# A one-core cross-attention and expert kernel: norms on ScalarE, first operand pairs on two queues, one gate transpose later, and an end in halves

## What is computed

```python
n = layernorm(x)                      # no weights: (x - mean) / sqrt(var + 1e-5)
q, k, v = n @ Wq.T + bq, ctx @ Wk.T + bk, ctx @ Wv.T + bv       # 16 heads of 8
A = where(causal, q @ k.T / sqrt(8), -inf)                      # per batch and head, 256 x 256
x = x + softmax(A) @ v @ Wo.T + bo
n = layernorm(x)
shared = sum_s gelu(n @ up_s.T) @ down_s.T                      # 2 experts of 64
p = softmax(n @ router.T); gate = p at its top 4 of 16, else 0
routed = sum_r (gate_r * gelu(n @ up_r.T)) @ down_r.T           # 16 experts of 64
x = x + shared + routed
```

## Time and profile before

| what | us |
|---|---|
| median of 3 runs | 215.53 |
| lowest, highest | 215.24, 215.61 |
| the profiled execution, its own time | 215.19 |
| its span in the trace | 213.4 |
| TensorE busy | 185.1 (87%) |
| VectorE busy | 170.2 (80%) |
| ScalarE busy | 141.7 (66%) |
| GpSimd busy | 96.6 (45%) |

### The profile page before, as it was taken

The page is one execution under the profiler, slowest core; times in us unless marked ns, Lnnn a source line. Parts: engine busy times, 40 slices in busy tenths (PEclk is TensorE's granted clock), DMA queues, the critical chain, the costliest instruction groups (busy, mean ns, idle before and its releaser), DMA issues.

```text
span 213.4 us, 4806 instructions
## 1 busy us (share of the span) xinstructions
PE 185.1 (87%) x1610; PEld 136.9 (64%) x1610; DVE 170.2 (80%) x456; ACT 141.7 (66%) x285; POOL 96.6 (45%) x184
## 2 busy tenths in 40 slices
PE   0539787998999899999999997899996989999991
PEld 0326564676677577767776774568884767677870
DVE  4667989978889999899899993349859759597881
ACT  4320265776778688766856778787787567968651
POOL 8559039948869676484575567601101010000000
PEclk9999999999999999999999999999999999999999
DMA  4474132742313313313213200100000001010001
GB/s 126 114 208 114 50 83 65 255 128 58 101 51 80 105 31 84 96 50 82 80 44 88 60 2 7 30 3 28 3 2 2 3 0 49 0 49 0 24 30 49
DMA packets 23736, 12.99 MB, mean 61 GB/s; under 512 B 4696, under 2 KB 23400, under 8 KB 23712
## 3 DMA queue, kind: packets, MB, share of 16 engines
q1 hardware_dynamic: 22288, 12.12, 20.5%
q10 hardware_dynamic: 1328, 0.53, 1.0%
q0 software_dynamic: 96, 0.03, 0.1%
HBM read 3.86 MB, written 1.05 MB: 23 GB/s over the span
## 4 chain that ended last, share of the span: by engine, by line
PE 47%; DVE 18%; issue 9%; POOL 6%; ACT 6%; DVEq 0%; ACTq 0%; POOLq 0%
DVE sb_mx L797 7%; PE psum L986 5%; PE psum L968 3%; PE psum L903 3%; PE psum L900 3%; PE psum L901 3%; PE psum L885 3%; PE psum L887 3%; PE psum L886 3%; PE psum L945 2%; POOL sb_probs L434 2%; PE psum L892 2%; PE psum L989 2%; POOL sb_x L441 2%; PE psum L952 2%
## 5 line engine op out<-in xcount | busy, mean ns | idle before, releaser
L597 ACT ACTIVATE sb_probs<-psum 128x512 f32<-128x512 f32 x96 | 55.8, 603 | 19.3 <-PE psum L968 18.3
L797 DVE TENSOR_REDUCE sb_mx<-psum 128x2 f32<-128x512 f32 (+1 forms) x96 | 62.5, 678 | 6.0 <-PE psum L952 3.6
L434 POOL TENSOR_SCALAR_AFFINE_SELECT sb_probs<-sb_probs 128x256 f32<-128x256 f32 (+1 forms) x96 | 45.3, 486 | 30.8 <-ACT sb_probs L597 29.9
L684 DVE TENSOR_TENSOR sb_probs<-sb_probs,psum 128x512 f32<-128x512 f32 x32 | 21.8, 682 | 10.9 <-ACT sb_probs L537 10.7
L537 ACT ACTIVATE sb_probs<-psum 128x512 f32<-128x512 f32 x36 | 21.4, 598 | 13.2 <-PE psum L887 13.0
L968 PE MATMUL psum<-sb_qk_op 128*128 128x256 bf16 x128 | 24.3, 272 | 2.2 <-DVE sb_bo L855 1.3
L945 PE MATMUL psum<-sb_qk_op 96*128 96x256 bf16 x128 | 25.7, 283 | 0.0
L691 DVE TENSOR_TENSOR sb_hid_l<-sb_probs,sb_hid_h 128x512 fp32r<-128x512 f32 x36 | 24.7, 686 | 0.3
L543 ACT CAST sb_hid_h<-sb_probs 128x512 fp32r<-128x512 f32 x36 | 22.2, 617 | 2.5 <-DVE sb_probs L684 2.3
L942 PE MATMUL psum<-sb_fut,sb_id_b 128*128 128x256 bf16 x64 | 18.2, 285 | 4.2 <-issue 3.6
L986 PE MATMUL psum<-sb_probs,sb_v_op 128*32 128x256 f32 x256 | 20.5, 391 | 1.2 <-ACT sb_o_raw L572 0.8
(11 more groups left out here) (114 smaller groups left out, 388.7 us busy)
## 6 DMA issues: line engine op xcount, KB each, us to landing
sb_qk_op<-sb_qk SPq DMA_DIRECT2D x90, 64.0 KB
sb_ctx<-in_ctx_t SPq DMA_DIRECT2D x8, 128.0 KB, 2.7
sb_num<-sb_o_raw SPq DMA_DIRECT2D x8, 128.0 KB, 2.1
out<-sb_o_raw SPq DMA_DIRECT2D x4, 256.0 KB, 2.3
sb_x<-in_x SPq DMA_DIRECT2D x3, 256.0 KB, 4.6
sb_up_f<-in_rup_t SPq DMA_DIRECT2D x1, 512.0 KB, 3.6
sb_dn_f<-in_rdown SPq DMA_DIRECT2D x1, 512.0 KB, 4.6
sb_qk_op<-sb_qk ACTq DMA_DIRECT2D x6, 64.0 KB
```

The source lines that it names most:

```text
L434: nc.gpsimd.affine_select(out=v, in_=v, compare_op=ALU.is_ge, fill=0.0, base=0, pattern=[[0, v.shape[1]], [1, P]], channel_multiplier=-1). ...
L597: nc.scalar.activation(probs[g][:, u * BANK:(u + 1) * BANK], psum[:, BANK_S + n % SB, :], ACT.Exp, scale=float(DH) ** -0.5).then_inc(s_exp, 1)
L684: nc.vector.tensor_tensor(hid[buf[k]], gel[buf[k]], psum[:, 3 + k % 2, :], ALU.mult)\
L797: nc.vector.tensor_reduce(dst, src, AX, ALU.max).then_inc(m_max, 1)
```

## The change

- **Norms.** The subtraction and multiplication of `apply_1` for q = 2, 3, 4 and of the second norm go from VectorE to ScalarE as ACTIVATE Identity with scale rs and bias shift = -mean * rs. GpSimd makes the shift in two more small operations behind its power. ScalarE does the second norm's pair behind the exponential of t = 2 (t = 4 from turn 10 on).
- **Pairs of batch 0.** SyncE and ScalarE's queue each issue three transfers of the first half and then three of the second.
- **bo_done** is waited for ahead of the first `pv` instead of the first `exp_unit`, and the product goes to another PSUM bank.
- **up of the first two chunks** is issued in turn 9 at t = 2 and t = 5, ahead of the chunks' remaining steps.
- **Gates of batch 6** are transposed and read at t = 6 of turn 11 instead of t = 2.
- **The end in halves.** The last tile's copy, transposes, addition and transfer are split in two; the second transfer is ScalarE's. SyncE's loop over transfers is written out.

The diff, without most of its context lines:

```diff
@@ -280,6 +283,10 @@
+        def rstd_steps(q):
+            return 2 * (q + 1) if q < 2 else 4 * q
@@ -340,6 +347,15 @@
                     sp.wait_ge(m_ps, 1)
+                if c == 0:
+                    sp.wait_ge(qk_hi, 2)
+                    pairs(sp, side, 0, 0)
+                    sp.wait_ge(qk_mid, 1)
+                    pairs(sp, side, 0, 1)
+                    sp.wait_ge(qk_lo, 1)
+                    pairs(sp, side, 0, 2)
+                    pairs(sp, side, 1, 1, 3, 2)
+                    return
@@ -417,8 +435,14 @@
                 nc.gpsimd.tensor_scalar(var1[:, tiles], mv1[:, tiles, 1], 1e-5, None, ALU.add).then_inc(rstd1, 1)
-                pool.wait_ge(rstd1, 2 * q + 1)
+                done = rstd_steps(q) - (2 if q < 2 else 4)
+                pool.wait_ge(rstd1, done + 1)
                 nc.gpsimd.tensor_tensor(rs1[:, tiles], var1[:, tiles], halfs[:, tiles], ALU.pow).then_inc(rstd1, 1)
+                if q >= 2:
+                    pool.wait_ge(rstd1, done + 2)
+                    nc.gpsimd.tensor_tensor(shift1[:, tiles], mv1[:, tiles, 0], rs1[:, tiles], ALU.mult).then_inc(rstd1, 1)
+                    pool.wait_ge(rstd1, done + 3)
+                    nc.gpsimd.tensor_scalar(shift1[:, tiles], shift1[:, tiles], -1.0, None, ALU.mult).then_inc(rstd1, 1)
@@ -461,8 +485,12 @@
                         nc.gpsimd.tensor_scalar(var2[:, :], mv2[:, :, 1], 1e-5, None, ALU.add).then_inc(rstd2, 1)
-                        pool.wait_ge(rstd2, count(2 * c + 1))
+                        pool.wait_ge(rstd2, 4 * c + 1)
                         nc.gpsimd.tensor_tensor(rs2[:, :], var2[:, :], halfs[:, 0:QB], ALU.pow).then_inc(rstd2, 1)
+                        pool.wait_ge(rstd2, 4 * c + 2)
+                        nc.gpsimd.tensor_tensor(shift2[:, :], mv2[:, :, 0], rs2[:, :], ALU.mult).then_inc(rstd2, 1)
+                        pool.wait_ge(rstd2, 4 * c + 3)
+                        nc.gpsimd.tensor_scalar(shift2[:, :], shift2[:, :], -1.0, None, ALU.mult).then_inc(rstd2, 1)
@@ -556,6 +584,12 @@
+            def apply_1(q):
+                act.wait_ge(rstd1, rstd_steps(q))
+                for a in range(*X_PARTS[q]):
+                    nc.scalar.activation(xn[:, a, :], x2[:, a, :], ACT.Identity, bias=shift1[:, a:a + 1],
+                                         scale=rs1[:, a:a + 1]).then_inc(xn_done, 1)
@@ -615,6 +649,13 @@
                     c = turn.batch(4)
+                    if t == late(turn, 2) and c is not None:
+                        act.wait_ge(rstd2, 4 * c + 4)
+                        for a in range(QB):
+                            nc.scalar.activation(xn2[:, a, :], x2[:, c * QB + a, :], ACT.Identity, bias=shift2[:, a:a + 1],
+                                                 scale=rs2[:, a:a + 1]).then_inc(xn2_done, 1)
+                    if (turn.at, t) in ((1, 4), (2, 1), (3, 1)):
+                        apply_1(turn.at + 1)
@@ -639,14 +680,17 @@
                         read_gates(c)
-                    if (turn.at, t) == (NB + 3, 2):
+                    if (turn.at, t) == (NB + 3, 6):
                         read_gates(NB - 2)
...
                         act.wait_ge(qk_hi, 2)
-                        pairs(act, 0, 1, 0)
+                        act.wait_ge(qk_mid, 1)
+                        pairs(act, 0, 0, 3, 4)
+                        act.wait_ge(qk_lo, 1)
+                        pairs(act, 0, 0, 5)
@@ -654,10 +698,7 @@
                 if turn.at == 0:
-                    act.wait_ge(qk_mid, 1)
-                    pairs(act, 0, 1, 1, 3, 4)
-                    act.wait_ge(qk_lo, 1)
-                    pairs(act, 0, 1, 2, 5)
+                    pairs(act, 0, 1, 0, 4, 5)
@@ -667,7 +708,12 @@
             high(NCT - 1, NCH - 1)
-            read_d(NCT - 1)
+            act.wait_ge(d_ps, NCT * NCH)
+            act.wait_ge(y_ps, NCT)
+            for h in range(2):
+                nc.scalar.copy(y_t[:, S * h:S * h + S], psum[:, 5, S * h:S * h + S]).then_inc(d_half[h], 1)
+            act.wait_ge(y_sum[1], 1)
+            act.dma_start(out_v[:, NTT - 2:NTT, :], y[:, 2:4, :]).then_inc(out_done, 16)
@@ -797,14 +843,6 @@
                             split_maxima(c, turn.side(1), t // 6)
-                    c = turn.batch(4)
-                    if t == late(turn, 1) and c is not None:
-
-                        dve.wait_ge(rstd2, count(2 * c + 2))
-                        for a in range(QB):
-                            nc.vector.tensor_scalar(xn2[:, a, :], x2[:, bass.ds(c * QB + a, 1), :].rearrange("p a e -> p (a e)"),
-                                                    mv2[:, a, 0:1], rs2[:, a:a + 1], ALU.subtract, ALU.mult)\
-                                .then_inc(xn2_done, 1)
@@ -843,8 +881,6 @@
                         stats_1(4)
-                    if (turn.at, t) in ((1, 4), (2, 1), (3, 1)):
-                        apply_1(turn.at + 1)
@@ -852,7 +888,7 @@
                     dve.wait_ge(bv_ps, 1)
-                    nc.vector.tensor_tensor(bo_sb[:, :], bo_sb[:, :], psum[:, BANK_S, 0:E], ALU.add).then_inc(bo_done, 1)
+                    nc.vector.tensor_tensor(bo_sb[:, :], bo_sb[:, :], psum[:, BANK_PV, 0:E], ALU.add).then_inc(bo_done, 1)
@@ -864,7 +900,12 @@
             low(NCT - 1, NCH - 1)
-            finish(NCT - 1)
+            dve.wait_ge(out_done, 16 * NCT)
+            for h in range(2):
+                dve.wait_ge(y_half[h], 1)
+                nc.vector.tensor_tensor(y[:, 2 * h:2 * h + 2, :],
+                                        psum[:, BANK_B - h, 0:S].rearrange("p (a e) -> p a e", e=E),
+                                        x2[:, NTT - 4 + 2 * h:NTT - 2 + 2 * h, :], ALU.add).then_inc(y_sum[h], 1)
@@ -881,10 +922,18 @@
                 w = slice(P * k, P * k + P)
+                if at == 0:
+                    pe.wait_ge(w_lo, 8)
+                    pe.wait_ge(xl_done, BANK // S)
+                    pe.wait_ge(m_max, UNITS * NB)
                 pe.wait_ge(u_gelu, count(at - UP_BANKS + 1))
...
                 mm(psum[:, k % UP_BANKS, :], up_l[:, w], xh[:, cols], start=False, stop=True).then_inc(u_ps, 1)
+            def spread_gates(n, k):
+                at = n * NCH + k
+                cols = bass.ds(n * BANK, BANK)
@@ -910,7 +959,9 @@
             def chunk(n, k, first):
-                up(n, k)
+                if n > 0 or k > 1:
+                    up(n, k)
+                spread_gates(n, k)
@@ -959,8 +1010,6 @@
                 pe.wait_ge(s_exp, count(UNITS * c + t - SB + 1))
-                if (c, t) == (0, 0):
-                    pe.wait_ge(bo_done, 1)
@@ -978,6 +1027,8 @@
                     pe.wait_ge(v_read, count(c + 1))
+                if (c, g) == (0, 0):
+                    pe.wait_ge(bo_done, 1)
@@ -1029,6 +1080,8 @@
                             transpose_maxima(turn, c, 1)
+                    if (turn.at, t) in ((NB + 1, 2), (NB + 1, 5)):
+                        up(0, t // 3)
@@ -1075,18 +1128,14 @@
                         transpose_gates(turn, c)
-                    if (turn.at, t) == (NB + 3, 2):
+                    if (turn.at, t) == (NB + 3, 6):
                         transpose_gates(Turn(NB + 2, NB + 2, NB), NB - 2)
...
                     if at == (0, 0):
-                        pe.wait_ge(w_lo, 8)
                         pe.wait_ge(spr_set, 4)
-                        pe.wait_ge(ff_in, 16 * 5)
-                        pe.wait_ge(xl_done, BANK // S)
                         pe.wait_ge(gt_read, BANK // S + 1)
-                        pe.wait_ge(m_max, UNITS * NB)
@@ -1106,9 +1155,9 @@
                     pe.wait_ge(bv_spread, 1)
-                    mm(psum[:, BANK_S, 0:E], bv_all[:, :], wo_sb[:, :], start=True, stop=True).then_inc(bv_ps, 1)
+                    pe.wait_ge(xnt_read, 3)
+                    mm(psum[:, BANK_PV, 0:E], bv_all[:, :], wo_sb[:, :], start=True, stop=True).then_inc(bv_ps, 1)
                     pe.wait_ge(ones_in, 32)
-                    pe.wait_ge(xnt_read, 3)
@@ -1127,7 +1176,12 @@
                 down(NCT - 1, k)
-            transpose_y(NCT - 1)
+            pe.wait_ge(y_done, NCT)
+            for h in range(2):
+                pe.wait_ge(d_half[h], 1)
+                for a in (2 * h, 2 * h + 1):
+                    last = nc.tensor.transpose(psum[:, BANK_B - h, P * (a % 2):P * (a % 2) + P], y_t[:, P * a:P * a + P], id_f[:, :])
+                last.then_inc(y_half[h], 1)
```

More of the change, by code:

```diff
@@ L218, in xattn_moe_kernel @@
         out_done, unused = sem("out_done"), sem("unused")
+        d_half, y_half, y_sum = ([sem(f"{name}{h}") for h in range(2)] for name in ("d_half", "y_half", "y_sum"))
         RSTEPS = 11
@@ L403, in _ @@
             attention(turn_of)
-            with sp.Fori(0, NCT) as n:
+            for n in range(NCT - 1):
                 sp.wait_ge(y_done, n + 2)
-                sp.dma_start(out_v[:, bass.ds(n * (BANK // P), BANK // P), :], y).then_inc(out_done, 16)
-            sp.wait_ge(out_done, 16 * (NCT + 1))
```

(5 more changed lines are left out.)

3 lines of the change are left out of this document (2 added, 1 removed).

## The result

| | kernel before | changed kernel |
|---|---|---|
| median of 20 runs, us | 215.5 | 218.12 |
| lowest | 215.17 | 216.77 |
| the profiled execution, its own time | 215.19 | 216.77 |
| its span | 213.4 | 215.0 |

The runs compared stand at a ratio of 1.0087, 95% interval 1.0065 to 1.011: the change makes the kernel slower by about 0.9%. The forecast was 215.4 us, within 0.2% of no change, with a range of 213.2 to 217.1; the median lies above it. The ratio leaves out five slow runs of the changed kernel, over 1.5% above its fastest (220.05 to 220.47 us); without them its median is 217.39. The two profiled executions differ by 1.58 us.

A forecast was written before the change was run, and what follows sets the result against it. TensorE was taken to bound turns 5 to 8 and the expert phase, latency chains the start and end. Terms -1.0 - 1.46 - 0.6 + 2.98 = -0.08 us gave 215.11; with 0.34 for the median, 215.4, range 213.2 to 217.1.

The forecast's parts named there:

- The pair of norms in turns 4 to 8: Transposes of xn2: TensorE waits 0.86 us for ScalarE's norms, 1.14 in turn 5; in all +2.98 us, bounds 2.0 to 4.1.
- I take 0.36 at a step of 0.25: Assumed duration and step, in us, of one 128x128 norm on ScalarE, placed between 128x32 and 128x256 ACTIVATE rows.
- the prediction's four terms: New time from the waits at the transposes of xn2 in turns 5 to 8: 1.04, 0.52, 0.30 and 0.76 us.
- What other waits swallow: TensorE's existing waits for VectorE absorb part of each new wait: about 0.1, 0.34 and 0.56 us in turns 5 to 7.
- its lost 0.36: Turn 4: new wait of 0.86 us, of which the old 1.02 us idle time was let swallow 0.5.
- The start: Up to turn 2: gain of 2.1 us at 28 us, partly lost on ScalarE and GpSimd; -1.0, of -2.1 to -0.3.
- Turn 3: Four norms delay L929 by about 0.9 us, taken by a 0.96 wait for VectorE at 50.04; 0, up to +0.4.
- The pairs: Batch 0's operand transfers, three issues on each of two queues: 0.5 us gained at the start, of 0.25 to 0.8.
- The row of six issues: One queue's six issues take 4.71 us from 9.85; preferred to a skill rule that would make the pairs' gain 0.
- Gates and end: Batch 6's gates lose their wait at 165.80, -1.46 us; the end in halves issues 0.54 earlier, -0.6 us.
- the slower one: Rival: norms at 473 ns make waits 1.1 us in five turns, half the start's gain goes; 217.1 us, chance 0.20.
- prices both norms at 0.41 from start to end: Alternative from a skill's ACTIVATE budget: wait at xn2's transposes 1.0 us instead of 0.86, sum above 0.7 us worse.

The follow-up runs named there:

- first experiment: The changed kernel with the second norm's pair back on VectorE and GpSimd's two operations for its shift gone: 213.32 us, ratio 0.9894 to the kernel before.

## Why the prediction was wrong, point by point

**The account.** Between the profiled executions the change was forecast at -0.08 us and measured at +1.58. Of the miss 1.04 lies at the start, 0.33 in turn 3 and 0.52 in turns 4 to 8; from turn 9 on the gain was 0.21 larger. The changed kernel's profiled execution, 216.77, lies inside the range. Its median of 20 lies 1.35 above that execution, where 0.34 was added for the kernel before: that part is the clock, which was in no term, and it carries the median out of the range.

**The bound and where to look**: right. TensorE bounds turns 5 to 8, VectorE got nothing back there (first experiment), and no wait but the one named arose at the transposes of xn2.

**The pair of norms in turns 4 to 8**: the mechanism was right, the term too small, 2.98 against 3.50. The step that failed is "I take 0.36 at a step of 0.25, between them and close to the plain 128x256 copy". It was 0.49 at 0.385; a copy was the wrong neighbour, since what costs is the number of pointers. The prediction's own sign of being wrong, norms over 0.47 us, came in. Each wait was thereby about 0.26 short: turns 5 to 8 lost 3.59 where the prediction's four terms give 2.62. What other waits swallow was judged rightly there (0.17, 0.40 and 0.62 in turns 5 to 7, for 0.1, 0.34 and 0.56). Turn 4 made up for nearly half of the shortfall, and that was luck: its lost 0.36 was -0.09, for the old wait of 1.02 is gone, and not 0.5 of it. In turns 10 and 11 the norms cost nothing, as forecast: from turn 9 on 82.29 us against 82.23 with all norms on VectorE.

**The start**: "-1.0 us, of -2.1 to -0.3" was +0.04, outside its range. Its gain was 0.36 short of the 2.1: TensorE's maxima come 1.74 earlier (VectorE's second split 1.23). Its loss was mis-sized: four norms are 1.54, not 1.0, and the selects that follow them could start only 0.21 earlier (30.84 for 31.05); GpSimd's row then lost 0.36 of idle time, not 0.5, and gained 0.6 of shift. These three, 0.36, 0.54 and 0.14, are the 1.04. The same wrong price stands in both big terms. No run took the later wait for the bias alone, so its share of the gain isn't shown. "ScalarE is nearly empty then" held for turn 1 and not for turn 2, where the same move put four norms ahead of an exponential.

**Turn 3**: "0, up to +0.4" was +0.33. The wait for ScalarE's norms there was 1.24, of which the old 0.96 swallowed most.

**The pairs**: 0.5 was taken, 0.7 measured in the only comparison where the first split isn't hit by GpSimd. The row of six issues was the better guide.

**Gates and end**: -1.46 - 0.6 was forecast, -2.09 measured (1.54 and 0.58 in the profiles), and -2.27 from turn 9 on in the changed kernel, with the early products in it.

**The rivals**: the slower one (wait of 1.1 us per turn, 217.1) had the right mechanism and nearly the right price and was given 0.20. It should have been the forecast. Its sum (+1.7 on the forecast) fits the profiles' 1.66 in part by luck: it put 1.2 on turns 4 to 8 and 0.5 on the start, and 0.52 and 1.04 were measured. The row of 473 ns for an ACTIVATE with one pointer was in hand, and I interpolated over the columns alone. Where the prediction prices both norms at 0.41 from start to end, its own times give a wait of 1.07 and not 1.0.

**The clock** was in no term; what is known of its part stands in the last section.

## What to carry to other kernels

Before work goes from a busy engine to one with slack, price the instruction in its own form (its pointers, its source, its step) and look at what is queued behind it in the receiving engine at that place: 3 to 4 us of slack per turn didn't help, since 0.77 us of it were wanted between two instructions that TensorE waits for. A norm moved to ScalarE paid in turn 1, where ScalarE stood idle, and cost in turns 2 to 8, where exponentials stood behind it. And when an experiment misses, look for a short instruction that got long, before the theory is given up: 1.0 us of gain was hidden in one 128x16 operation.
